# A hybrid block on one core: side work of TensorE in 46 placed pieces, weighted low parts on GpSimd, the last two y summed on TensorE

## The reference

```python
x = x + attn(ln(x))   # xn = rms_norm(ln(x)); 16 causal heads of 16; returns xn + out @ Wo.T + bo
x = x + ffn(ln(x))    # base + shared low rank (16) + 6 routed experts of rank 16, the top 2, weighted
x = x + ssm(ln(x))    # conv of 4 taps, silu, delta, B, C; 16 states: h = decay*h + dt*x*B; y = sum h*C; gate; @ Wo
x = x + ffn(ln(x))    # the same ffn again
```

## Time and profile before

| | us |
|---|---|
| median of 3 runs | 2282.9 (2281.12 to 2284.76) |
| profiled execution | 2291.34 |
| its span | 2289.6 |
| VectorE busy | 1833.3 (80%), 2805 instructions |
| TensorE busy | 1788.5 (78%), 10753 matmuls |
| ScalarE busy | 1291.8 (56%) |
| GpSimd busy | 1041.5 (45%) |
| mean granted clock of TensorE | 0.902 |

### The profile page before, as it was taken

One profiled execution on the slowest core, in us unless ns is written; L12 is line 12 of the kernel. 1 busy time (PEld: TensorE's weight loads), 2 busy tenths in 40 slices (PEclk: granted clock), 3 DMA queues, 4 the chain that ended last, 5 costly groups with the idle time before them and its releaser, 6 DMA issues. The chain is left out here.

```text
span 2289.6 us, 31493 instructions
## 1 busy us (share of the span) xinstructions
PE 1788.5 (78%) x10753; PEld 1088.8 (48%) x10784; DVE 1833.3 (80%) x2805; ACT 1291.8 (56%) x2259; POOL 1041.5 (45%) x658
## 2 busy tenths in 40 slices
PE   4779787888888797878888797888888797856333
PEld 2445444545454554545454454645454554534122
DVE  5444779879897988979787988879888988879783
ACT  2445656575756566665756556565756556553431
POOL 1010544545454554535454644545454645444441
PEclk8889898999999898999999998999999899976766
DMA  3212676657666666757566665666666666533331
GB/s 110 79 56 66 125 142 136 154 124 157 126 134 144 134 148 139 156 119 155 127 128 145 142 148 130 149 133 141 139 130 152 137 138 140 116 87 80 74 83 37
DMA packets 188353, 283.91 MB, mean 124 GB/s; under 512 B 33809, under 2 KB 125986, under 8 KB 188194
## 3 DMA queue, kind: packets, MB, share of 16 engines
q1 hardware_dynamic: 155650, 163.40, 29.2%
q0 software_dynamic: 32544, 118.50, 27.5%
HBM read 128.72 MB, written 34.08 MB: 71 GB/s over the span
## 5 line engine op out<-in xcount | busy, mean ns | idle before, releaser
L1195 POOL TENSOR_TENSOR inp<-u,b_all 128x1024 f32<-128x1024 f32 x256 | 616.4, 2408 | 656.6 <-DVE hc L1035 568.9
L1035 DVE TENSOR_TENSOR_SCAN hc<-dec,inp 128x1024 f32<-128x1024 f32 x256 | 627.8, 2453 | 4.2 <-ACT dec L799 3.0
L708 ACT ACTIVATE pt<-bank 128x512 f32<-128x512 f32 x640 | 383.7, 601 | 373.3 <-PE bank L342 369.7
L317 PE MATMUL bank<-sk,sq 96*128 96x512 bf16 (+3 forms) x1024 | 281.7, 314 | 175.4 <-DVE mall L916 95.4
L799 ACT ACTIVATE dec<-dt,a_neg 128x511 f32<-128x511 f32 x512 | 338.8, 722 | 60.2 <-DVE hc L1035 60.1
L1042 DVE TENSOR_TENSOR hc<-hc,bank 128x1024 f32<-128x1024 f32 x240 | 290.8, 1212 | 58.8 <-PE bank L488 57.1
L1203 POOL DMA_DIRECT2D y<-hc x210 | 184.7, 880 | 299.1 <-DVE hc L1042 236.6
L340 PE MATMUL bank<-sq,sk 98*128 98x512 bf16 (+3 forms) x1024 | 282.7, 315 | 37.4 <-ACT parts L727 25.5
L916 DVE TENSOR_REDUCE mall<-bank 128x1 f32<-128x512 f32 x256 | 172.1, 672 | 125.0 <-PE bank L319 123.9
L317 PEld LDWEIGHTS bank<-sk,sq 96*128 96x128 bf16 x1024 | 102.5, 100 | 303.5 <-DVE mall L916 116.3
L918 DVE TENSOR_REDUCE mall<-bank 128x4 f32<-128x512 f32 x256 | 174.7, 682 | 72.3 <-PE bank L319 69.4
(11 more groups left out here) (151 smaller groups left out, 3221.2 us busy)
## 6 DMA issues: line engine op xcount, KB each, us to landing
y<-hc POOLq DMA_DIRECT2D x226, 512.0 KB, 5.6
b_all<-b_kept SPq DMA_DIRECT2D x256, 256.0 KB, 4.3
qk_parts<-parts SPq DMA_DIRECT2D x96, 256.0 KB, 2.5
sq<-qk_parts SPq DMA_DIRECT2D x384, 64.0 KB, 3.9
sk<-qk_parts SPq DMA_DIRECT2D x384, 64.0 KB, 4.0
X<-in_x SPq DMA_DIRECT2D x16, 512.0 KB, 6.4
out<-X SPq DMA_DIRECT2D x16, 512.0 KB, 4.5
sq<-hlt SPq DMA_DIRECT2D x256, 2.0 KB
```

The costliest lines, as they stand in the source:

```text
L317: mm(dst[:, o:o + n], sq[0:KS, slot, h, qb * P:(qb + 1) * P], sk[0:KS, slot, h, 0:n], start=True, stop=False)
L708: A(pt[:, n % PT, :], score_bank[unit % 2][:, :], ACT.Exp).then_inc(exp_done.sem, 1)
L1035: V.tensor_tensor_scan(h, d, v, 0.0, ALU.mult, ALU.add).then_inc(scan_done.sem, 1)
L1195: G.tensor_tensor(inp[:, n % 2, :, :], u[:, :, :], b_all[:, k % 3:k % 3 + 1, :].to_broadcast([P, C, T]), ALU.mult).then_inc(inp_ready.sem, 1)
```

## The change

Positions are now given as half units: now = 2 (10 q + p), plus 1 behind the unit's own work. A table for each engine says at which offset from 80a a piece for element a is issued; due(now, at) yields that element. Offsets of one period differ by multiples of 80: 126 is unit (2,3) ahead, of the element behind; -28 is unit (2,6) ahead, of the element in front. In the old numbering TensorE's pieces stood at xn (-74, -74), qk0 -50 to -45, v (-28, -27), qk1 -8 to -3, ao and x1 (95, 95, 96, 97), the first turn (107, 107), low 109, hw 124, up (126, 127), xs (138, 138), conv (140, 141), gate (142, 143), bc 146, 148, 150, dt (147, 149), x3 (250, 251), second turn (262, 262), low 264, hw 276, up (278, 279).

Each piece now has its own bank (BANK), its own position and its own waits; both halves of a turn, a residual addition and a copy may lie apart. norm_f goes from 105 to 103, norm_s from 136 to 131, delta from 153 to 155, gated from 245 to 246, rsqrt_l from behind the step of unit 7 (255) to ahead of it (253). GpSimd's weighing and its residual addition, before at (0,8) and (1,1), are both at -57. The multiplication of the low-rank parts by the weights goes from VectorE to GpSimd (weigh_low, at 111 and 268); the weights get a buffer for each FFN. The product with C of a group's second state goes from unit 3 to 4, head_norm from 5 to 4. The y of the last two elements is summed in PSUM by TensorE, through an identity matrix, in banks that the attention no longer uses; the paired additions and the DMAs for them go. store waits for the additions at 279 and 282, and stays at unit (2,0). The decay exponents are formed later, on ScalarE alone.

```diff
-    LS = 8
+    LK = 32
...
-    PRODUCT_AT = {1: 0, 3: 1, 6: 2, 8: 3}
-    DECAY_AT = {0: -1, 3: 0, 5: 1, 8: 2}
-    PAIRED = NB - 2
-    FIRST, END = -6, NQ + 11
+    PRODUCT_AT = {1: 0, 4: 1, 6: 2, 8: 3}
+    DECAY_AT = {1: -1, 4: 0, 5: 1, 8: 2}
+    LATE = NB - 2
+    FIRST, END = -6, NQ + 12
+
+
+    FRAME = 2 * UN * NG
+    PE_AT = {"xn": (-76, -71), "qk00": (-52, -50, -48), "qk01": (-49, -47, -44), "v": (-29, -34),
+             "qk10": (-8, -5, -4), "qk11": (-5, -3, -1), "ao": (92, 94), "x1": (96, 97), "turn0": (105, 107),
+             "low0": 109, "hw0": 122, "up0": (125, 126), "xs": (135, 135), "conv": (137, 141), "gate": (146, 140),
+             "bc": (149, 151, 154), "dt": (148, 149), "x3": (251, 251), "turn1": (260, 262), "low1": 264, "hw1": 275,
+             "up1": (278, 280)}
+    BANK = {"xn": (0, 1), "qk00": 0, "qk01": 1, "v": (1, 1), "qk10": 0, "qk11": 1, "ao": (1, 1), "x1": (1, 0),
+            "turn0": (1, 1), "low0": 1, "hw0": 1, "up0": (1, 0), "xs": (1, 0), "conv": (1, 1), "gate": (1, 0),
+            "bc": 1, "dt": (0, 0), "x3": (1, 0), "turn1": (1, 0), "low1": 0, "hw1": 0, "up1": (1, 0)}
+    ACT_AT = {"norm_q": -97, "norm_f": 103, "exp0": 116, "norm_s": 131, "softplus": 152, "decays": 160,
+              "norm_l": 257, "exp1": 266, "xn": (-75, -70), "qk00": (-52, -50, -47), "qk01": (-50, -49, -44),
+              "v": (-29, -34), "qk10": (-9, -6, -4), "qk11": (-5, -3, -1), "ao": (92, 95), "turn0": (105, 107),
+              "low0": 110, "hw0": 120, "xs": (135, 138), "conv": (140, 141), "gate": (146, 140),
+              "bc": (149, 151, 154), "dt": (147, 150), "turn1": (261, 263), "low1": 264, "hw1": 275}
+    DVE_AT = {"add_x1": (94, 96), "stats_f": 98, "in0": 111, "out0": 117, "add_up0": (125, 125), "stats_s": 127,
+              "silu": 143, "delta": 155, "gated": 246, "add_x3": (251, 251), "stats_l": 252, "in1": 265, "out1": 267,
+              "add_up1": (279, 282), "stats_q": -100}
+    POOL_AT = {"weigh": -57, "residual": -57, "rsqrt_f": 99, "rsqrt_s": 122, "rsqrt_q": -104, "inputs": 151,
+               "rsqrt_l": 253, "low": (111, 268)}
+    SP_AT = {"parts": (-42, -3), "load_x": -109, "store_b": 144, "store": 280}
+    HEADS_PE, HEADS_DVE = 4, 4
...
+        side = {(name, j): (MA, MB)[BANK[name][j]] for name in ("xn", "v", "ao", "x1", "xs", "conv", "gate", "dt", "x3")
+                for j in range(2)}
+        side.update({("qk", j, s): (MA, MB)[BANK[f"qk{j}{s}"]] for j in range(2) for s in range(2)})
+        side.update({(name, f, j): (MA, MB)[BANK[f"{name}{f}"][j]] for name in ("turn", "up") for f in range(2)
+                     for j in range(2)})
+        side.update({(name, f): (MA, MB)[BANK[f"{name}{f}"]] for name in ("low", "hw") for f in range(2)})
+        side["bc"] = (MA, MB)[BANK["bc"]]
...
+        def late_banks(s):
+            return score_bank if s % 2 else max_bank
+        def due(now, at):
+            a, rest = divmod(now - at, FRAME)
+            return a if rest == 0 and has(a) else -1
...
+            def sum_y(k):
+                s, n = divmod(k, NS)
+                if has(s) and s >= LATE:
+                    if n == 0:
+                        pe.wait_ge(exp_done.sem, exp_done.at(NQ - 1))
+                        pe.wait_ge(mx_done.sem, mx_done.at(NQ - 1))
+                    pe.wait_ge(hc_done.sem, hc_done.at(s, n + 1))
+                    for c, m in enumerate(late_banks(s)):
+                        last = mm(m[:, :], ident[:, :], hc[:, k % HC, c, :], start=(n == 0), stop=(n == NS - 1),
+                                  skip_group_check=True)
+                    last.then_inc(y_summed.sem, 1)
...
-            def prepare_next(b, r, p, j):
-                if has(b + 1):
-                    if (r, p, j) == (0, 3, 0):
-                        turn_xn(b + 1)
-                    elif (r, p) in ((1, 5), (3, 6)):
-                        project_qk(b + 1, r // 2, j)
-                    elif (r, p) in ((1, 6), (3, 7)):
...
+            def side_work(now):
+                for j in range(2):
+                    if (a := due(now, PE_AT["x3"][j])) >= 0:
+                        ssm_out(a, j)
+                    if (a := due(now, PE_AT["turn1"][j])) >= 0:
+                        ffn_turn(a, 1, y_tok(a), j)
...
                     if p in PRODUCT_AT:
                         spread_c(k + PRODUCT_AT[p])
+                        sum_y(k + PRODUCT_AT[p] - 1)
                     if 0 <= q - 1 < NQ:
                         if p == 0:
                             values_b(q - 1)
                         elif p == 1:
                             values_c(q - 1)
-                        elif p == 4:
+                        if p == HEADS_PE:
                             turn_heads(q - 1)
                     if p == 7 and 0 <= q < NQ:
                         values_a(q)
-                    after_ssm(b - 3, r, p, 1)
-                    after_attention(b - 1, r, p, 1)
...
             def store(l):
-                sp.wait_ge(MB.free, MB.at("up", 1, l, 0))
-                sp.wait_ge(MA.free, MA.at("up", 1, l, 1))
+                for j in range(2):
+                    sp.wait_ge(side["up", 1, j].free, side["up", 1, j].at("up", l, 1, j))
...
-                V.tensor_tensor(wts[:, :, 1:], rank[:, :, :], red[:, 3, :, None].to_broadcast([P, TB, E]),
-                                ALU.mult).then_inc(dve_own.sem, 1)
-                dve.wait_ge(dve_own.sem, dve_own.one())
-                V.tensor_tensor(hw[:, f, :, 0:ER].rearrange("p t (e r) -> p t e r", r=R),
-                                low[:, f, :, 0:ER].rearrange("p t (e r) -> p t e r", r=R),
-                                wts[:, :, :, None].to_broadcast([P, TB, E + 1, R]),
-                                ALU.mult).then_inc(hw_done[f].sem, 1)
+                V.tensor_tensor(wts[:, f, :, 1:], rank[:, :, :], red[:, 3, :, None].to_broadcast([P, TB, E]),
...
+                    elif old_n == 0:
                         dve.wait_ge(hc_done.sem, hc_done.at(old_s, 1))
-                    elif old_s < PAIRED:
+                    else:
                         dve.wait_ge(y_added.sem, y_added.at(old_s, old_n))
-                    elif old_n % 2 and old_n < NS - 1:
-                        dve.wait_ge(pair_done.sem, pair_done.at(old_s - PAIRED, old_n // 2 + 1))
-                    else:
-                        dve.wait_ge(pair_added.sem, pair_added.at(old_s - PAIRED, (old_n + 1) // 2))
                     h, d, v = (t.rearrange("p c t -> p (c t)")
...
-                    if s >= PAIRED and n and n % 2 == 0:
-                        dve.wait_ge(hc_done.sem, hc_done.at(s, n + 1))
-                        V.tensor_tensor(hc[:, k % HC, :, :], hc[:, k % HC, :, :], hc[:, (k - 1) % HC, :, :],
-                                        ALU.add).then_inc(pair_done.sem, 1)
...
             def gate_y(l):
-                if l < PAIRED:
+                if l < LATE:
                     dve.wait_ge(y_added.sem, y_added.at(l))
+                    V.scalar_tensor_tensor(y[:, l % 2, :, :], gate[:, l % 2, :, :], 1.0, y[:, l % 2, :, :], ALU.add,
+                                           ALU.mult).then_inc(yg_done.sem, 1)
                 else:
-                    dve.wait_ge(pair_added.sem, pair_added.at(l - PAIRED))
-                V.scalar_tensor_tensor(y[:, l % 2, :, :], gate[:, l % 2, :, :], 1.0, y[:, l % 2, :, :], ALU.add,
-                                       ALU.mult).then_inc(yg_done.sem, 1)
+                    dve.wait_ge(y_summed.sem, y_summed.at(l - LATE))
+                    for c, m in enumerate(late_banks(l)):
+                        last = V.scalar_tensor_tensor(y[:, l % 2, c, :], gate[:, l % 2, c, :], 1.0, m[:, :], ALU.add,
+                                                      ALU.mult)
+                    last.then_inc(yg_done.sem, 1)
...
+            def weigh_low(b, f):
+                pool.wait_ge(wts_done[f].sem, wts_done[f].at(b))
+                G.tensor_tensor(hw[:, f, :, 0:ER].rearrange("p t (e r) -> p t e r", r=R),
+                                low[:, f, :, 0:ER].rearrange("p t (e r) -> p t e r", r=R),
+                                wts[:, f, :, :, None].to_broadcast([P, TB, E + 1, R]),
+                                ALU.mult).then_inc(hw_done[f].sem, 1)
...
-            def add_pair(s, n):
...
+                if (a := due(now, POOL_AT["rsqrt_l"])) >= 0:
+                    rsqrt(a, KIND_L)
+                if (a := due(now, POOL_AT["rsqrt_f"])) >= 0:
+                    rsqrt(a, KIND_F)
+                if (a := due(now, POOL_AT["rsqrt_s"])) >= 0:
+                    rsqrt(a, KIND_S)
+                if (a := due(now, POOL_AT["rsqrt_q"])) >= 0:
+                    rsqrt(a, KIND_Q)
+                for f in range(2):
+                    if (a := due(now, POOL_AT["low"][f])) >= 0:
+                        weigh_low(a, f)
+                if (a := due(now, POOL_AT["weigh"])) >= 0:
+                    weigh(a)
```

(6 more changed lines are left out.)

636 lines of the change are left out of this document (315 added, 321 removed).

## The result

The changed kernel took 2246.2 us (median of four runs, 2245.9 to 2248.0). The kernel before, run on the same chip, took 2283.8 us (2281.1 to 2287.4). The ratio is 0.984, with a 95% interval from 0.982 to 0.985: 37.6 us are gained where 93 were forecast. The spans of the two profiled executions, 2289.6 and 2244.3 us, differ by more, 45.3 us, because the profiled execution of the kernel before was 7.5 us above its median.

What follows compares the result with a forecast made beforehand. TensorE and VectorE, neither full, were taken to bound the kernel by turns, at most two units apart. Twelve periods 60, ramp 13 and tail 20 us sum to 93; 2291 - 93 = 2198, less 8: 2190 us, range 2105 to 2275.

Steps and rivals of the forecast that it cites:

- Heap A: TensorE's side work from unit (2,6) to (3,5), where VectorE waits 11.3 us; reordering gains 4 us a period, 2 to 6.
- Heap B: Units (1,1) to (1,5), TensorE waiting for y and tok_f; earlier rsqrt and norm_f gain 3 us a period, 1.5 to 4.
- Softplus: delta behind one scan removes a 0.8 us wait a period; later u may make gated wait, 0.5 us.
- Exclusion: GpSimd's moved work holds up VectorE at scan (2,0), 1.7 us, and the router, 2; with gated's 0.5, 4 us a period.
- Low parts on GpSimd: VectorE loses two products of 0.625 us a period, gaining 1.25 us.
- The sentence that stood beside the sum: By the rule that VectorE and GpSimd exclude one another alone, the 1.25 us, 20 over the run, would be worth nothing.
- Sum in a period: Steady stretch: 4 + 3 + 0.8 + 1.25 - 4 = 5 us gained for one element; u to u 124 us.
- Tail: Last two elements: y summed on TensorE, rsqrt earlier, shorter wait before the last y; 20 us gained, 8 to 35.
- Ramp: First two elements and the one before the tail: 13 us gained.
- the gain is eaten: Rival: ScalarE, ahead of TensorE at hw0 and dt0, delays scores; only tail and a little remain, about 2255 us, chance 0.15.

Runs made afterwards that it cites:

- The first experiment: Changed kernel with ScalarE's softplus at 154 instead of 152, behind the last copy of B/C: 2216.3 us, ratio 0.970.
- e8_no_softplus: Changed kernel with VectorE's gating and second-FFN two-input operations moved from behind the scans, GpSimd's second low part at 270, softplus still at 152: 2190.9 us, 0.957.
- e6_places: Changed kernel with softplus at 154, VectorE's gating and second-FFN two-input operations moved from behind the scans, GpSimd's second low part at 270: 2167.4 us, 0.950.
- b1_tail: Kernel before with only the last two y summed by TensorE in PSUM, without paired additions and their DMAs: 2268.4 us, 0.993.
- b3_v_early: Kernel before with only v one unit earlier, (2,5) instead of (2,6), on TensorE and ScalarE: 2270.4 us, 0.993.
- e4_three: Changed kernel with softplus at 154, weighing at -64 and residual at -58, first FFN's low part at 118: 2210.3 us, 0.968.

## Why the prediction was wrong

The sign was right, the size was not: 37.6 us for 93. Point by point, by the steps of the sum:

**Heap A, 4 us a period.** The mechanism was there, the size was not. v ahead of the late keys was given 3.0 us; alone on the kernel before it was worth 0.4 us a period in the steady stretch, which is no more than executions differ by. The term took what TensorE does while it would stand, and not what VectorE gets of it. In the changed kernel heap A's waits of VectorE did fall from 11.3 to 4.6 us, more than forecast; that the spreading of the other pieces did this is argued, no run here has it alone. But 3.94 + 0.91 us of new waits stand right behind it, those of softplus. The cost that was feared for the keys (2.6 us by the store on SP's queue) didn't show: TensorE's waits for them fell by half, from 22.0 to 10.6 us in twelve periods.

**Heap B, 3 us.** Undersized. The two places alone gave 4.6 us a period: 3.9 us of VectorE's waits, the upper end of the 1.5 to 4 forecast, and 0.6 us less of busy time. TensorE's shorter busy time at the higher granted clock (106.1 against 108.9 us) was not in the sum.

**Softplus, 0.8 us gained and 0.5 to pay.** This step failed: what softplus holds up was put at nothing beyond delta and the gating. The wait of 0.8 us did go, but what stands behind softplus in ScalarE's list was not looked at. The prediction named ScalarE places that are ahead of TensorE's (hw0, dt0) as a rival; it did not name the copy of B/C at 154, behind softplus at 152 with 4.7 us of work, on whose bank TensorE's last projection waits. The first experiment put it at 2.4 us a period net, 31 us in all; with good places 17. Most of the stand stayed even then, 3.76 us behind another copy.

**Exclusion, 4 us.** This step failed too, by its size: where the sum had 1.7 + 2 = 3.7 us for it, some 7 us were measured (14.5 against 7.5 us above the least durations), and that is after the 1.4 us that line 956 gave back, which the sum did not have either. The prediction priced it by what GpSimd was newly given: weigh_low in front of a scan, weigh and residual side by side. It is VectorE's instruction that counts, at what place and behind what. The prediction wrote of router_in and router_out that their small operations read SBUF twice, and then priced them at up to 4 us for everything; each of the three took 2 us or more at one of the two FFNs of a period, 5.3 us more than before in all. And the gating of y, moved to a place with only a maximum between a scan and it, went from 2.13 to 3.07 us. e8_no_softplus, with the places alone, took 6.8 us of VectorE's busy time away and 3.6 us off the period; with the softplus moved too, e6_places, the period fell by 6.9. So the gain of the closed waits was eaten, but on VectorE beside GpSimd's instructions and by a copy behind softplus, and not by ScalarE's stands at hw0 and dt0 as that rival had it.

**Low parts on GpSimd, 1.25 us gained.** The sign was wrong: 1.8 us a period lost in the changed kernel, nothing gained or lost with good places. The sentence that stood beside the sum, that the shift would be worth nothing, was the better forecast.

**Sum in a period.** 129.1 - 5 = 124.1 was forecast and 129.08 measured; above 127, the prediction said, would prove it wrong. Waits -6.5, busy +5.5 leave a period a little over 1 us shorter by VectorE's account; the trace's four periods are 128.9 against 130.3, while over twelve they are equal (waits -4.6, busy +5.0).

**Tail, 20 us.** Undersized: 35.7 us in the period before the last and the stretch behind the last u. The sum of y alone measured 16 (10 + 2.5 forecast), the rsqrt moved forward about 4 (5 forecast), and the 5.78 us stand is gone in the changed kernel as forecast. The other 15 or so are put down to the places, which here have little work beside them, and the clock: the f32 products of the sum fill TensorE's gaps there, and what follows runs at the upper of its two levels (2.4 GHz; granted 1.00 from 2206 to 2216 us); b1_tail, with the sum alone, has the higher slices too. Its first groups of the output projection after y took 1.91 and 1.61 us before, at 2252.34 and 2254.26 us, after TensorE had stood for 11.84 us and at a granted clock of 0.50; now all four take 1.03 us, from 2209.13 us on. How the 15 us divide was not measured.

**Ramp, 13 us.** 12.0 by the first u, right in size; some 10 of it is v's place (b3_v_early).

The range (2105 to 2275) holds 2246, but not by its mechanism: the term that made 60 of the 93 us gave nothing, and 35.7 us in the tail for 20 stood in for a part of it. The rival nearest to what happened is that the gain is eaten, at 2255.

Three things stay open. First, the three edits of e4_three gave 36 us where their reasons added to 115, and the same softplus move gives 31 us alone and 17 on top of the places; why they overlap is argued (whoever is late hides the other), not shown. Second, at 122.2 us the best version has 109.1 us of VectorE and 105.3 us of TensorE in a period: 13 us are left, of which the trace shows 11.5 + 9.2 + 8.1 + 8.1 = 36.9 us in four periods as VectorE's four largest waits. Third, in that version, too, TensorE stands 3.75 us a period at line 344 for ScalarE's copy behind softplus (once at 1075.70 us); no run moves softplus behind that one as well.

## What to carry to other kernels

After instructions are moved, go through VectorE's instructions on SBUF, one by one, the smallest too, those with two inputs first but not alone (a one-input instruction of 128x4 was hit here), and ask which GpSimd instruction is let go just before each starts: a 24-column product then costs a whole GpSimd product. In these runs VectorE's instruction had to move; moving GpSimd's passed the cost on. For each matmul that reuses a bank, look at what stands on the reading engine between the bank's filling and its last reader, table loads included, and then at the next such matmul, on which the wait may land. And try the two or three places with the best reasons alone first: here two of them gave 60 us and the whole rebuilt order 37.6, and the repaired order 115.

## What the runs showed of the hardware

A VectorE product of 128x24 took 0.18 us alone and 2.08 us beside GpSimd's 128x1024 product; one of 128x144 took 0.30 and 2.03. The length was that of GpSimd's rest, not of its own. A VectorE tensor_scalar of 128x4 with a single SBUF input was hit as well: 1.57 us beside GpSimd's product at 780.12 us of the kernel before, 0.17 alone. A product with one input in PSUM was not: line 1042 took 1.20 to 1.22 us inside a GpSimd product too. Taking the conflict from one VectorE instruction by moving GpSimd's put it on another (line 1043 from 1327 to 308 ns, line 1013 from 170 to 452).

After its stand of 4.55 us TensorE's next group of four f32 matmuls took 3.75 us, where the same group without a stand took 1.96 us: it ran at the lower of the two levels, granted 0.50 from 1243.5 to 1250 us. So that stand cost 4.55 us and another 1.8 behind it. In the tail the reverse was seen: behind the sums of y, TensorE's groups took 1.03 us instead of 1.91. ScalarE's change of tables took 1.28 us each way around a logarithm of 1.06 us.
